# First norm, second tanh and second division of the first attention layer: who computes them, and when

## What is computed

```python
h = _layernorm(x, axis=-1) * (1 + ca) + sa
q = jnp.tanh(einsum('btd,hdo->btho', h, W_Q)) * (PI / 4)      # 16 heads, one value each
k = jnp.tanh(einsum('btd,hdo->btho', h, W_K)) * (PI / 4)
V = einsum('btd,hde->bthe', h, W_V)                           # 16 heads x 64
heads = cos(q) * cumsum(cos(k) * V, axis=1) + sin(q) * cumsum(sin(k) * V, axis=1)
denom = cos(q) * cumsum(cos(k), axis=1) + sin(q) * cumsum(sin(k), axis=1) + 1e-6
x = x + ga * einsum('deh,bthe->btd', W_O, heads / denom)
```

## Time and profile before

| | |
|---|---|
| device time, median of 3 runs | 1744.17 us (1740.03 to 1744.47) |
| the profiled execution, its own time | 1743.46 us |
| span of its profile | 1741.7 us, 38208 instructions |
| busy: TensorE / VectorE / ScalarE / GpSimd | 88% / 64% / 52% / 70% |
| first norm | to about 66 us |
| attention loop of the first layer | about 73 to 395 us |

### The profile page before, as it was taken

How to read it: one execution, slowest core, us unless ns; L and a number is a source line. 1 busy time by engine, 2 the same in 40 slices (tenths; PEclk the granted TensorE clock), 3 DMA queues, 4 the chain that set the end, 5 groups by cost and what they waited for, 6 DMA issues and landing times.

```text
span 1741.7 us, 38208 instructions
## 1 busy us (share of the span) xinstructions
PE 1529.0 (88%) x13596; PEld 1145.4 (66%) x13596; DVE 1119.5 (64%) x1777; ACT 909.7 (52%) x2313; POOL 1221.5 (70%) x1024
## 2 busy tenths in 40 slices
PE   6799999986999999999999967877877767699998
PEld 5456666565788888888888853433333326599997
...
GB/s 219 20 30 119 142 135 139 124 35 326 77 96 122 112 108 122 110 110 119 101 186 151 107 188 53 1 28 31 31 43 43 91 152 194 141 259 253 259 262 150
DMA packets 148049, 217.34 MB, mean 125 GB/s; under 512 B 48904, under 2 KB 108576, under 8 KB 142752
## 3 DMA queue, kind: packets, MB, share of 16 engines
...
...
## 4 chain that ended last, share of the span: by engine, by line
PE 54%; POOL 20%; DVE 8%; issue 7%; DMA 5%; ACT 1%; POOLq 0%; DVEq 0%; ACTq 0%; SPq 0%
PE ps L829 51%; POOL BIG L2547 16%; DMA BIG<-HB,BIG 5%; DVE BIG L1419 4%; PE ps L946 1%; POOL BIG L2731 1%; POOL BIG L2732 1%; POOL XD L2721 1%; DVE BIG L2032 1%; PE ps L1127 1%; ACT BIG L2081 1%; DVE bnst L1426 1%; POOL BIG L2709 1%; PE ps L1196 0%; POOL out L2721 0%
## 5 line engine op out<-in xcount | busy, mean ns | idle before, releaser
L829 PE MATMUL ps<-BIG 128*128 128x256 f16 (+9 forms) x11168 | 1230.7, 285 | 122.8 <-DVE BIG L2010 49.2
L829 PEld LDWEIGHTS ps<-BIG 128*128 128x128 f16 (+3 forms) x11168 | 940.9, 100 | 382.4 <-DVE BIG L2010 77.8
L2547 POOL TENSOR_TENSOR BIG<-BIG 128x256 f16<-128x256 f32 (+7 forms) x550 | 728.5, 1499 | 221.8 <-ACT BIG L2081 207.6
L2081 ACT ACTIVATE BIG<-BIG 128x512 f16<-128x512 f32 (+3 forms) x527 | 318.1, 661 | 225.5 <-DVE BIG L1419 160.5
L1419 DVE TENSOR_TENSOR BIG<-BIG 128x512 f16<-128x512 f32 (+12 forms) x345 | 258.6, 758 | 209.7 <-ACT BIG L2081 166.6
L2081 ACT ACTIVATE BIG<-ps 128x64 f32<-128x64 f32 (+7 forms) x663 | 232.1, 424 | 210.0 <-PE ps L1127 114.1
L1419 DVE TENSOR_TENSOR BIG<-ps,BIG 128x512 f32<-128x512 f32 (+3 forms) x389 | 285.3, 811 | 13.9 <-PE ps L829 12.5
L1419 DVE TENSOR_TENSOR BIG<-BIG,ps 128x512 f32<-128x512 f32 (+2 forms) x149 | 95.6, 642 | 185.9 <-PE ps L829 160.7
L2032 DVE TENSOR_REDUCE BIG<-BIG 128x160 f32<-128x2560 f32 x64 | 186.5, 2915 | 0.0
L2721 POOL DMA_INDIRECT XD<-BIG x67 | 113.2, 1690 | 85.2 <-DVE BIG L1916 81.4
L2709 POOL DMA_INDIRECT BIG<-HB,BIG x106 | 113.4, 1070 | 50.6 <-issue 26.4
...
## 6 DMA issues: line engine op xcount, KB each, us to landing
...
```

The source lines that it names most:

```text
L829: return e.matmul(o, lhsT, rhs, start=start, stop=stop, skip_group_check=True)
L2081: return e.activation(o, i, ACT.Copy)
L2547: return e.tensor_tensor(o, a, b, op)
```

## The change

1. Tiles 24 to 31 are normalised by VectorE (a TENSOR_SCALAR, subtract mean and multiply), in their tick behind the modulation of tile t - 3, instead of by ScalarE. TensorE waits for them by another semaphore, `n_xn`, which the second layer's norm also uses and whose numbers there are moved by eight.
2. Tile 1's values are no longer projected in tick 35 but behind the last tick.
3. ScalarE does the second tanh ahead of the copies of `spread_hi(0)`.
4. VectorE copies the key sums of tiles 16 to 31 out of bank 7 in pass 0 (`sums_out`, signalled by `kc`, a name for the semaphore `cT_ps`, which one instruction at the start has used up to 1). The turn of the heads waits for this copy. The six steps of the second division then work in SBUF, two each behind the adds of passes 1, 2 and 3.
5. TensorE's first cumulative sums wait for two steps of the first division (those that read bank 0), not for all six.

```diff
@@ -222,7 +222,10 @@
 
         T_ROUND, T_PIECES = (4, 14, 15, 18, 19), (5, 16, 24)
 
-        T_TANH, T_KEYS, T_SUMS, T_VALUES = 25, 30, 31, (33, 35)
+        T_TANH, T_KEYS, T_SUMS, T_VALUES = 25, 30, 31, (33,)
+
+        N_XN = 24
+        s["kc"] = s["cT_ps"]
 
         AHEAD, C_FIRST = 8, 3
 
@@ -926,13 +929,17 @@
                                        kk == 0 and p == 0, kk == 1 and p == 2)
                         m.then_inc(s["qk_ps"], 1)
                     if k == 2:
-                        pe.wait_ge(s["xn"], n + 1)
+                        if n < N_XN:
+                            pe.wait_ge(s["xn"], n + 1)
+                        else:
+                            pe.wait_ge(s["n_xn"], n - N_XN + 1)
                         if n >= 2:
                             pe.wait_ge(s["v_d"], 2 * n - 2)
                         for kk in range(2):
                             m = e.transpose(ps[6 + n % 2][:, kk * 128:(kk + 1) * 128], xn0[n % 6][:, kk * 128:(kk + 1) * 128], ident[:, :])
                         m.then_inc(s["xT_ps"], 1)
 
+            values(1)
 
             def turn_heads(i):
                 for q in range(2):
@@ -941,7 +948,7 @@
                         pe.wait_ge(s["ht_lo"], 2 * (i - 1) + q + 1)
                     else:
                         pe.wait_ge(s["v_d"], 2 * NT)
-                        pe.wait_ge(s["dn"], 12)
+                        pe.wait_ge(s["kc"], 2)
                     for j in range(4):
                         m = e.transpose(ps[6 + q][:, j * 128:(j + 1) * 128], TM[i % 2][:, 0, (4 * q + j) * 128:(4 * q + j + 1) * 128], ident[:, :])
                     m.then_inc(s["hdT_ps"], 1)
@@ -960,7 +967,7 @@
             for i in range(NT):
                 if i == 0:
 
-                    pe.wait_ge(s["dn"], 6)
+                    pe.wait_ge(s["dn"], 2)
                     pe.wait_ge(s["gr"], 4)
                     pe.wait_ge(s["th"], 4)
                 else:
@@ -1256,7 +1263,7 @@
                     if n % 2:
                         pe.wait_ge(s["n_xa"], n // 2 + 1)
                     else:
-                        pe.wait_ge(s["n_xn"], n // 2 + 1)
+                        pe.wait_ge(s["n_xn"], NT - N_XN + n // 2 + 1)
                     if n >= 2:
                         by, k = vr_by(n - 2)
                         pe.wait_ge(s[by], k)
@@ -1470,26 +1477,40 @@
                     dve.wait_ge(s["ck_hi"], 2 * h + j + 1)
                     tt(cks[:, 1, j, cut], src[:, cut, 16:32], cks[:, 0, j, cut], ALU.subtract).then_inc(s["ck_lo"], 1)
 
-            def divide(h):
+            def sums_out():
+
+                dve.wait_ge(s["kc_ps"], 2)
+                dve.wait_ge(s["th"], 6)
+                e.tensor_copy(TH[:, 16:32, :].rearrange(FLAT), ps[7][:, :]).then_inc(s["kc"], 1)
+
+            def divide(h, ops=range(6)):
 
                 cut = slice(16 * h, 16 * h + 16)
-                cumc, cums = (cumb[h][:, j].rearrange("p b c n -> p (b c) n") for j in range(2))
                 dn, d2 = (TH[:, cut, :].rearrange(FLAT)[:, 256 * k:256 * k + 256].rearrange("p (t n) -> p t n", n=16) for k in range(2))
-                dve.wait_ge(s["kc_ps"], h + 1)
+                if h:
+                    cumc, cums = dn, d2
+                    dve.wait_ge(s["kc"], 2)
+                else:
+                    cumc, cums = (cumb[h][:, j].rearrange("p b c n -> p (b c) n") for j in range(2))
+                    dve.wait_ge(s["kc_ps"], 1)
 
                 dve.wait_ge(s["th"], 3 * h + 3)
-                c = Serial(dve, s["dn"], 6 * h)
-                tt(dn, QC[:, cut, 0:16], cumc, ALU.mult).then_inc(c.next(), 1)
-                n = c.next()
-                tt(d2, QS[:, cut, 0:16], cums, ALU.mult).then_inc(n, 1)
-                n = c.next()
-                e.scalar_tensor_tensor(out=dn, in0=dn, scalar=1e-6, in1=d2, op0=ALU.add, op1=ALU.add).then_inc(n, 1)
-                n = c.next()
-                e.reciprocal(dn, dn).then_inc(n, 1)
-                n = c.next()
-                tt(QC[:, cut, 0:16], QC[:, cut, 0:16], dn, ALU.mult).then_inc(n, 1)
-                n = c.next()
-                tt(QS[:, cut, 0:16], QS[:, cut, 0:16], dn, ALU.mult).then_inc(n, 1)
+                for n in ops:
+                    if h or n:
+                        dve.wait_ge(s["dn"], 6 * h + n)
+                    if n == 0:
+                        o = tt(dn, QC[:, cut, 0:16], cumc, ALU.mult)
+                    elif n == 1:
+                        o = tt(d2, QS[:, cut, 0:16], cums, ALU.mult)
+                    elif n == 2:
+                        o = e.scalar_tensor_tensor(out=dn, in0=dn, scalar=1e-6, in1=d2, op0=ALU.add, op1=ALU.add)
+                    elif n == 3:
+                        o = e.reciprocal(dn, dn)
+                    elif n == 4:
+                        o = tt(QC[:, cut, 0:16], QC[:, cut, 0:16], dn, ALU.mult)
+                    else:
+                        o = tt(QS[:, cut, 0:16], QS[:, cut, 0:16], dn, ALU.mult)
+                    o.then_inc(s["dn"], 1)
 
             for i in range(AHEAD):
                 ahead(i)
@@ -1510,6 +1531,10 @@
                         for kk in range(2):
                             e.tensor_scalar(vr0[n % 5][:, kk, :], ps[6 + n % 2][:, kk * 128:(kk + 1) * 128], modT[:, 0, 2 + kk, b:b + 1],
                                             modT[:, 0, kk, b:b + 1], ALU.mult, ALU.add).then_inc(s["v_d"], 1)
+                    if k == 0 and n >= N_XN:
+                        dve.wait_ge(s["rs_v"], n // 4 + 1)
+                        dve.wait_ge(s["xT_ps"], n - 5)
+                        xnorm(xn0[n % 6], n).then_inc(s["n_xn"], 1)
 
 
             def spread(i):
@@ -1582,7 +1607,9 @@
                 dve.wait_ge(s["rd"], 4 * i + 4)
                 tt(tm[:, 0], tm[:, 0], tm[:, 1], ALU.add).then_inc(s["hd"], 1)
                 if i == 0:
-                    divide(1)
+                    sums_out()
+                if 1 <= i <= 3:
+                    divide(1, range(2 * i - 2, 2 * i))
                 if i % 4 == 1 and i > 1:
                     factor(8 + i // 4 - 1, row(i - 2))
                 if i >= R_AFTER:
@@ -2139,7 +2166,7 @@
                     if k == 4:
                         act.wait_ge(s["v_d"], 2 * n + 2)
                         copy(hTh[:, :, n * 128:(n + 1) * 128], vr0[n % 5]).then_inc(s["hi"], 1)
-                    if k == 0:
+                    if k == 0 and n < N_XN:
                         xnorm(n)
 
 
@@ -2198,9 +2225,10 @@
                 w = cv_width(l, c)
                 copy(pr[c % 2][0][:, 0:w], st[c % 2][:, 0:w]).then_inc(s["cv_hi"], 1)
 
+            keys(1, 0)
             spread_hi(0)
-            for step in range(3):
-                keys(1, step)
+            keys(1, 1)
+            keys(1, 2)
             spread_hi(1)
             for i in range(NT):
                 if i % 4 == 0 and i:
```

## The result

| | kernel before | changed kernel |
|---|---|---|
| median of 5 runs each, us | 1741.35 (1740.03 to 1744.47) | 1733.45 (1730.75 to 1734.12) |
| ratio, 95% interval | | 0.9948 (0.9936 to 0.9960) |
| profiled execution, its span, us | 1743.46, 1741.7 | 1730.75, 1729.0 |

The change makes the kernel 0.52% faster, 9.1 us by the ratio (the medians lie 7.9 apart). Two later comparisons of the same pair gave 0.9948 (0.9933 to 0.9964) and 0.9961 (0.9949 to 0.9973).

A forecast was written before the change was run, and what follows sets the result against it. The chain of waits gave TensorE 54%, GpSimd 20%, VectorE 8%. Third pass's sums 5.89 us earlier (0.64 of it before the loop's first products), less 0.63 for the division, made -5.26: forecast 1738.5 us, range 1735.5 to 1742.1.

The forecast's parts named there:

- Part 1: First norm, tiles 24 to 31 moved to VectorE: K and S stay, so it pays nothing by itself.
- K: Moment VectorE has the low parts of the first keys, 57.90 us before; forecast move -0.8 to +1.1, taken as 0.
- S: Moment of VectorE's first spread (tile 0's first products), 66.75 us before; forecast to stay there.
- Part 2: Step into the loop, tanh and tile 1's values change places: loop's first products 0.64 us earlier, at 76.85 (bounds 0.2 to 0.8).
- Part 3: Pass 0 to pass 1, second division moved out: third pass's cumulative sums at 92.31, 5.89 us before 98.20.
- Part 4: Division steps behind the adds of passes 1 to 3: pass 2's 2.44 exceeds the 1.81 cover, costing +0.63 us.
- The clock falls all the same: Rival, loop's pass 1: TensorE's gaps keep the clock low, 1.70 comes back, -3.56, 1739.9; chance 0.14.
- One long hold: Rival, first norm: one VectorE norm ahead of K held 3.5 us more, -1.8, 1741.7; chance 0.10.
- No slack in the loop: Rival, loop passes 1 to 3: all 4.5 us of the division falls on the path, -1.4, 1742.1; chance 0.07.
- GpSimd wins every time: Rival, first norm: VectorE's norms lose to every ready GpSimd instruction, K up to 7.3 later, +2.1, 1745.6; chance 0.05.

The follow-up runs named there:

- c_only: Kernel before with only the second division from a copy, two steps each behind the adds of passes 1 to 3; ratio to before 0.9959.
- after_nonmr: Changed kernel without the two small VectorE instructions that make the negated means of tiles 24 to 31; ratio to the kernel before 0.9947.
- no_a: Changed kernel with all 32 norms back on ScalarE, the other changes kept; ratio to the kernel before 0.9973, run again 0.9969.

## Why the prediction was wrong

**Part 1, K.** Taken as no move, with 57.1 to 59.0 as bounds; it was 56.17. What failed is the sum of durations. I added 0.72 for a pair of copies and 0.40 for a norm, 1.12 a tile; the rows are 0.96 apart (49.73 to 50.69), since an instruction starts some 0.08 before the recorded end of the last. Six tiles of that are 0.96; VectorE was also free 0.56 earlier (49.09 for 49.65; that is the execution's earlier statistics, not the change), and two norms ahead of K were held 0.57 together, where I had allowed up to 1.3: 57.1 - 0.96 - 0.56 + 0.57 = 56.2. The key sums came 1.9 earlier, of which 1.0 is left at S: tile 0's values began at 59.61 instead of 61.54, but the clock was at its lower level until 61.4 (in before until 61.5, when they began), so their group took 3.78 where before had 2.90. Half of that 1.0 was the execution's, whose statistics were 0.54 early. Behind the statistics K came 1.19 earlier and S, with the clock alike, 0.70.

**Part 2.** The tanh came at 66.19, cumulative sums at 72.20 behind GpSimd, mechanism as foretold. But the term of -0.64 was on the wrong side: by the stretch from S to the loop's first products it is +0.36 (11.10 for 10.74). That these products still stood at 76.81, where I had 76.85, is luck: S was 1.04 early, half of it by the norms that I had put at nothing and half by the execution. I had allowed the hold on the keys' low parts 0.1 to 0.6, and it is 1.0, with 0.23 more on the division's sum (0.92 for 0.69). GpSimd's string moves forward with the change, into VectorE's two-input instructions; that was the part to follow.

**Part 3.** Right in each step: copy at 82.90 (82.9), turn of heads at 84.44 (84.5) in 1.04, clock 1.00, third pass's sums at 92.25 (92.31). The part is worth 5.27 by its stretch, for the forecast's 5.25; c_only's lead has 5.1.

**Part 4.** +0.63 taken, 0 found. Sum and reciprocal need 2.12 (100.10 to 102.22 in the rows below), not 2.44: the sum takes 0.42, and the 0.69 that I took for it came from a row beside a string of GpSimd (68.19 to 72.87). What is left over, the 0.23 by which the projection's products are late (5.95 before 107.94 would be 101.99), is swallowed by VectorE's short wait for TensorE ahead of the next eight products (0.16 in pass 1, none in pass 2).

```profile
100.10 0.42 DVE L1506 SCALAR_TENSOR_TENSOR BIG<-BIG 128x256 f32<-128x256 f32 x1
100.55 1.75 DVE L1508 RECIPROCAL BIG<-BIG 128x256 f32<-128x256 f32 x1
102.22 0.41 DVE L1426 TENSOR_TENSOR ps<-ps,BIG 128x256 f32<-128x256 f32 x1
```

The errors cancelled: forecast was 5.26 (5.89 less 0.63), found 5.27 + 0.70 - 0.36 = 5.6 from the parts and leads of 5.4 to 5.6 at the end of the loop.

**The sum.** The step that failed is the sentence behind the sum: "the loop's passes and the later stages are the same instructions, each started by the one before ... so it stays". The instructions are the same, but not the clock that they meet: it saved 1.67 us more at pass 30, which makes 7.1 at the routing. I had the 0.50 window at 90 as proof of what a low stretch costs, and looked for other such places only within the region of the change; the 4.45 row stood in the trace of before. The second error was the base. The runs shown were 1740.03, 1744.17 and 1744.47, the profiled one 1743.46; I subtracted from those near 1744, while five runs have 1741.35. From that base -5.26 gives 1736.1, and -7.1 gives 1734.2, beside 1733.45 measured. Of the 5 us between forecast and time the base is 2.4 and the clock 1.7; moved down by the first alone the range would just have held the time (from 1733.1), by the second alone not quite (from 1733.8). Of the rest, 1.0, the parts have 0.3, and what remains can't be told from scatter.

**Rivals.** The clock falls all the same: not in three traces of the changed kernel; once in no_a, where it cost 1.34 and not 1.70. One long hold: the 3.86 stayed where it was, and where it fell on a norm (after_nonmr) it cost nothing more, as it ends with GpSimd's string. No slack in the loop: refuted; only unsplit does the division cost, 3.1. GpSimd wins every time: it wins a whole string once, until 49.15, and later a single instruction at a time. The Trainium skill, page "SBUF — State Buffer", section "SBUF: two separate sides", gives the shared port to whoever starts first, for a whole instruction. The exclusion agrees with the traces. The "one instruction" agrees only in part. In the long hold VectorE waited through five or six of GpSimd's, which follow each other every 0.63 us, to the end of the string (49.15). But in later strings of the same trace three norms got through in 0.74 to 0.90, and the two low parts at 75.11 ended at 76.88 inside a string that lasts until 79.01:

```profile
53.68 8.77 POOL L2575 TENSOR_TENSOR BIG<-BIG 128x256 f16<-128x256 f32 x12 [2.00 <-ACT BIG L2108]
...
74.14 4.87 POOL L2575 TENSOR_TENSOR BIG<-BIG 128x512 f16<-128x512 f32 x4 [2.08 <-ACT BIG L2108]
```

What makes the first hold long stays open; after_nonmr shows only that it isn't the small instruction.
